# Small gaps inside the SBUF buffers that TensorE reads, in an attention and FP4 block on one core

## What is computed

```python
x  = L0_attn_src
xn = _layernorm(x, axis=-1)
# attention, per head: Q = elu(xn @ Wq + bq) + 1, K the same with Wk, v = xn @ Wv + bv
KV = jnp.einsum('bshd,bshm->bhdm', K, v)
Z  = 1.0 / (jnp.einsum('bshd,bhd->bsh', Q, K.sum(axis=1)) + EPS)
o  = jnp.einsum('bshd,bhdm,bsh->bshm', Q, KV, Z).reshape(b, s, H * DH)
x1 = _layer_norm(xn + o @ Wo + bo, g1, be1)
y  = jax.nn.gelu(x1 @ W1 + b1, approximate=False) @ W2 + b2
s  = _layer_norm(x1 + y, g2, be2)
# gated part; fp4_linear rounds both operands, blockwise
h  = jax.nn.silu(fp4_linear(xn, w_gate)) * fp4_linear(xn, w_up)
g  = _silu(fp4_linear(h, w_down))
out = x + s * g
```

## The kernel before, in words

| step | moving | columns | stationary | matmuls of `mm3` in all |
|---|---|---|---|---|
| `q_proj`, Q | `xnTh`, `xnTl` | 512 | `wqh`, `wql` | 768 |
| `at_step`, attention out | `Mh`, `Ml` | 256 | `RH[j]`, `RL[j]` | 1536 |
| `h_proj`, hidden layer | `xTh`, `xTl` | 512 | `w1h`, `w1l` | 768 |
| `f_step`, second layer | `w2h`, `w2l` | 256 | `RH[j]`, `RL[j]` | 1536 |
| `gate_up` | `wgh`, `wgl` | 352 | `xqh`, `xql` | 1536 |
| `down` | `wdh`, `wdl` | 256 | `hqh`, `hql` | 960 |

## Time and profile before

### The profile page before, as it was taken

The page is one execution under the profiler, slowest core; times in us unless marked ns, Lnnn a source line. Parts: engine busy times, 40 slices in busy tenths (PEclk is TensorE's granted clock), DMA queues, the critical chain, the costliest instruction groups (busy, mean ns, idle before and its releaser), DMA issues.

```text
span 1678.5 us, 30547 instructions
## 1 busy us (share of the span) xinstructions
PE 1644.1 (98%) x11105; PEld 1469.2 (88%) x11105; DVE 1322.8 (79%) x2587; ACT 967.5 (58%) x1754; POOL 778.4 (46%) x718
## 2 busy tenths in 40 slices
PE   7999999999999999999999999999999999999997
PEld 6878888888889898989999998989898999999897
DVE  6685664555879797979889797979797988979797
ACT  6665656655464646565655556464646565555644
POOL 4564543434134444444453534444444446353446
PEclk9999999999999999999999999999999999999999
DMA  7322323422200101021010102010101201010100
GB/s 230 130 77 89 106 66 116 121 91 91 93 1 1 51 1 51 19 86 52 1 51 2 51 2 104 2 51 2 51 19 34 77 29 51 1 51 2 51 1 26
DMA packets 69986, 89.36 MB, mean 53 GB/s; under 512 B 8383, under 2 KB 54603, under 8 KB 68814
## 3 DMA queue, kind: packets, MB, share of 16 engines
q1 hardware_dynamic: 69838, 87.42, 15.9%
HBM read 53.30 MB, written 34.10 MB: 52 GB/s over the span
## 4 chain that ended last, share of the span: by engine, by line
PE 54%; DVE 12%; issue 4%; ACT 1%; POOL 1%; DVEq 0%; ACTq 0%
PE QH L81 7%; PE QH L83 6%; PE QH L82 6%; PE AC L81 6%; PE AC L83 6%; PE AC L82 6%; PE GU L81 4%; PE GU L83 4%; PE GU L82 4%; PE TT L816 3%; DVE hb L1760 1%; DVE bslna L1840 1%; DVE hb L1758 1%; PE QH L714 1%; DVE AC L1831 1%
## 5 line engine op out<-in xcount | busy, mean ns | idle before, releaser
L1212 ACT ACTIVATE rh<-QH 128x512 fp32r<-128x512 f32 x256 | 147.1, 595 | 84.2 <-DVE QH L1918 80.1
L81 PE MATMUL GU<-wgh,xqh 128*128 128x352 f32 x512 | 171.2, 334 | 8.9 <-DVE hb L1760 8.8
L2416 POOL TENSOR_TENSOR hb<-hb,rs_h 128x704 f32<-128x704 f32 x64 | 89.1, 1392 | 170.0 <-DVE rs_h L1767 170.0
L82 PE MATMUL GU<-wgl,xqh 128*128 128x352 f32 x512 | 165.7, 324 | 0.0
L83 PE MATMUL GU<-wgh,xql 128*128 128x352 f32 x512 | 165.6, 323 | 0.0
L1933 DVE TENSOR_TENSOR rl<-QH,rh 128x512 fp32r<-128x512 f32 x128 | 85.7, 689 | 95.1 <-ACT rh L1212 74.7
L81 PE MATMUL AC<-Mh,rh 128*128 128x256 f32 x512 | 145.7, 285 | 0.0
L81 PE MATMUL AC<-w2h,rh 128*128 128x256 f32 x512 | 144.2, 282 | 0.0
L82 PE MATMUL AC<-Ml,rh 128*128 128x256 f32 x512 | 142.8, 279 | 0.0
L83 PE MATMUL AC<-Mh,rl 128*128 128x256 f32 x512 | 142.7, 279 | 0.0
L82 PE MATMUL AC<-w2l,rh 128*128 128x256 f32 x512 | 142.4, 278 | 0.0
(11 more groups left out here) (241 smaller groups left out, 5711.1 us busy)
## 6 DMA issues: line engine op xcount, KB each, us to landing
xa<-in_L_attn_src SPq DMA_DIRECT2D x16, 512.0 KB, 4.2
xt_scratch<-xth SPq DMA_DIRECT2D x32, 256.0 KB, 2.6
xt_scratch<-xtl SPq DMA_DIRECT2D x32, 256.0 KB, 3.0
xb<-in_L_attn_src SPq DMA_DIRECT2D x16, 512.0 KB, 4.2
xnTh<-xt_scratch SPq DMA_DIRECT2D x32, 256.0 KB, 4.7
xnTl<-xt_scratch SPq DMA_DIRECT2D x32, 256.0 KB, 5.4
out<-x SPq DMA_DIRECT2D x15, 512.0 KB, 6.6
m_scratch<-mh SPq DMA_DIRECT2D x16, 256.0 KB, 2.4
```

Of the source, the lines that this page charges most:

```text
L81: e.matmul(outp, lh, rh, start=start, stop=False, skip_group_check=check)
L82: e.matmul(outp, lh, rl, start=False, stop=False, skip_group_check=check)
L1212: e.activation(RH[j % 4][:], src, ACT.Copy).then_inc(S[sem], 1)
L2416: e.tensor_tensor(hb, hb, spread(rs_h[i % 2][:], 44), ALU.mult).then_inc(S["hin"], 1)
```

## The change

The buffers that TensorE reads get unused bytes inside. A new helper `spaced` allocates rows of `n + gap` numbers and hands out the first `n` of each. `gap` is in float32 numbers, so that 8 is 32 bytes. The slots of the two rings become 520 numbers long, of which 512 are used. `main_rest` shrinks from 682 to 562 numbers, since the space after it is full.

```diff
+        def spaced(name, k, n, gap):
+
+            return sb(name, [128, k, n + gap], F32R)[:, :, 0:n]
+
         sb("before_weights", [128, 24])
-        wqh, wql = sb("wqh", [128, 2, 1024], F32R), sb("wql", [128, 2, 1024], F32R)
-        w1h, w1l = sb("w1h", [128, 2, 1024], F32R), sb("w1l", [128, 2, 1024], F32R)
-        w2h, w2l = sb("w2h", [128, 8, D], F32R), sb("w2l", [128, 8, D], F32R)
-        wgh, wgl = sb("wgh", [128, 2, 1408], F32R), sb("wgl", [128, 2, 1408], F32R)
-        wdh, wdl = sb("wdh", [128, 6, D], F32R), sb("wdl", [128, 5, D], F32R)
+        wqh, wql = spaced("wqh", 2, 1024, 0), spaced("wql", 2, 1024, 0)
+        w1h, w1l = spaced("w1h", 2, 1024, 8), spaced("w1l", 2, 1024, 0)
+        w2h, w2l = spaced("w2h", 8, D, 0), spaced("w2l", 8, D, 0)
+        wgh, wgl = spaced("wgh", 2, 1408, 8), spaced("wgl", 2, 1408, 0)
+        wdh, wdl = spaced("wdh", 6, D, 0), spaced("wdl", 5, D, 0)
         sb("after_weights", [128, 8])
...
-        xnTh, xnTl = sb("xnTh", [128, 2, 512], F32R), sb("xnTl", [128, 2, 512], F32R)
+        xnTh, xnTl = spaced("xnTh", 2, 512, 16), spaced("xnTl", 2, 512, 8)
...
-        xqh, xql = sb("xqh", [128, 2, D], F32R), sb("xql", [128, 2, D], F32R)
+        xqh, xql = spaced("xqh", 2, D, 8), spaced("xql", 2, D, 24)
...
-        sb("main_rest", [128, 682])
+        sb("main_rest", [128, 562])
...
-        xTh, xTl = sb("xTh", [128, 2, 512], F32R), sb("xTl", [128, 2, 512], F32R)
+        xTh, xTl = spaced("xTh", 2, 512, 0), spaced("xTl", 2, 512, 8)
         Gb = sb("Gb", [128, 4, D])
-        RH = [sb(f"rh{i}", [128, 512], F32R) for i in range(4)]
-        RL = [sb(f"rl{i}", [128, 512], F32R) for i in range(4)]
-        hqh, hql = sb("hqh", [128, 6, 128], F32R), sb("hql", [128, 6, 128], F32R)
+        RH = [sb(f"rh{i}", [128, 520], F32R)[:, 0:512] for i in range(4)]
+        RL = [sb(f"rl{i}", [128, 520], F32R)[:, 0:512] for i in range(4)]
+        hqh, hql = spaced("hqh", 6, 128, 8), spaced("hql", 6, 128, 0)
```

## The result

The changed kernel takes 1687.39 us, the median of five runs (1686.94 to 1689.59), against 1679.61 us. The ratio is 1.0045, 95% interval 1.003 to 1.006: slower, by 7.8 us. The span of the profiled execution is 1685.5 us, 7.0 us longer.

What follows compares the result with a forecast made beforehand. TensorE, busy 98% of the span, was taken as the bound. Gains of 3.0 + 3.1 + 1.5 = 7.6 us, 74% of them reaching the end, gave 5.6 us less: 1674.0 us, range 1663 to 1687.

Steps and rivals of the forecast that it cites:

- The place: TensorE's matmuls, whose paces from start to start were expected to change with the distances between their operands.
- what reaches the end: Share of TensorE's gain that shortens the whole time: 74%, since 26% of a group runs through VectorE and ScalarE.
- The copies: Copies into `hqh`, `xqh` and `xql`, now written in several pieces: cost 0, at most 0.5 us before a waiting TensorE.
- the first phase: Opening matmuls of 512 columns, 226.4 ns each: distances stay 0, cost 0.
- The sign: Whole kernel: faster, 5.6 us less, with chances faster 0.49, same 0.22, slower 0.29.
- `f_step` and `down`: Their 2624 matmuls of 256 columns: no change, bounds 6.9 us more and 4.6 us less on TensorE.
- `at_step`: Its 1344 slow matmuls of 256 columns: 3.0 us less on TensorE, bounds 5.9 less and 0.8 more.
- `q_proj`: Its 768 matmuls of 512 columns go from 233.3 to 229.2 ns: 3.1 us less on TensorE.
- `gate_up`: Its 1536 matmuls of 352 columns: 1.5 us less on TensorE, bounds 6.6 less and 6.3 more.
- `h_proj`: Its 768 matmuls of 512 columns: no change, bounds 2.2 us less and 3.1 us more.
- The slower rival: Mixed distances break the good pace in `f_step`, `down`, `h_proj`: 10.0 us more on TensorE, 1687.0 us; chance 0.30.
- Nothing happens: Matmul paces depend on when a burst starts, not on addresses: time stays 1679.6 us; chance 0.20.

Runs made afterwards that it cites:

- the rings alone: Kernel before the change with only the ring slots lengthened to 520 numbers, 512 of them used; 1684.47 us, ratio 1.0029.
- the low parts moved: Kernel before the change with `Ml` and `w2l` 64 bytes further from `Mh` and `w2h`; one run, 1686.4 us against 1680.37.
- the steady 0: Kernel before the change with 64 unused bytes ahead of the rings, giving `at_step`, `f_step` and `down` distance 0 modulo 128; 1688.28 us, ratio 1.0047.
- the exchange of `q_proj` and `h_proj`: Kernel before the change with their distances exchanged, `q_proj` steady at 64 and `h_proj` at 96 modulo 128; 1682.99 us, ratio 1.0025.

## Why the prediction was wrong

*The place* was right, and so was what reaches the end: only TensorE's matmuls changed, in the mean of a step by some 3 ns at most, and 70% of it reached the span where I had 74%. The copies cost nothing, and the first phase kept its pace.

*The sign was wrong, and the step that failed is the one on `f_step` and `down`*: "I take no change, since half of the slots get distances like the good ones and half do not". They cost 5.4 and 3.4 us of busy time, half of the 17.6 us between the 7.6 less that I had on TensorE and the 10.0 more that came. Most of the other half is the gain of 7.6 us in `at_step`, `q_proj` and `gate_up`, of which at most 0.8 came; `h_proj` adds 2.4. I had counted 0 among the good distances because the first phase, with 512 columns, has it. At 256 columns 0 is bad, steady or not: 119.4 and 118.9 ns. So are 32 (119.1) and 96 (119.3). The distance that all of these steps had before, 64, is the only one of the four at which a whole step was seen at 113.3 ns: at 0, 32 and 96 no single `at_step`, `f_step` or `down` has a mean under 117 ns in the runs with a steady distance or with the rings alone. Three slots in four lost it.

*`at_step`*, 3.0 us less: 0.6. It rested on the distance modulo 256, "every second one is of the kind that `down` has". That is true of slot 1 alone, since the other slots no longer have 64 modulo 128; and moving `Mh` by 128 bytes, alone, changed nothing.

*`q_proj`*, 3.1 us less: 0.4 by the means, 0.2 in busy time. A steady distance of 64 or 0 does give 2.3 to 3.1 ns. The changed kernel keeps 96 in half of the product and mixes 0 and 32 in the other.

*`gate_up`*, 1.5 us less: 2.2 more by the means, 0.6 in busy time. *`h_proj`*, no change: 2.5 us more; both steady 96 and 0 (with 128 modulo 256) cost it about as much as the mixture.

*The slower rival* named the steps `f_step`, `down` and `h_proj`, 10.0 us on TensorE and 1687.0 us; busy time rose by 10.0 and the time is 1687.39. The places were right. That the sum meets the tenth is luck: the three cost 11.2, and the other matmuls gave back 1.2. Its reason, that a changing distance keeps the streams from settling, is half of it. The run with the low parts moved shows, as far as one run can, that such a mixture harms; the rings alone and the steady 0 show that a wrong distance harms as much with no mixture within a step. My chances gave it 0.30 against 0.42, and counted against it that "within one slot of the ring the distance modulo 128 stays". That was a true objection to its reason, and none to its time.

*Nothing happens* falls: in the exchange of `q_proj` and `h_proj`, the paces went with the distances. What I had drawn from the rule of the Trainium skill, "TensorE: Matmul & The Clock Gate", section "Step-by-step: what each phase is for", on the two independent read ports, falls with it: that the addresses would not matter at all. Whether the rule itself fails, that the load of the next weights takes nothing from the matmul that streams, no run here shows, since it is still inference that it is this load which the stream meets. In the kernels with a steady distance the stationary operand of a matmul and that of the next have the same address modulo 128, so that the two can't be told apart, and none was run that could.

Also open is what one step hands to the next. `at_step` went from 117.1 to 114.8 ns when modulo 128 only `q_proj` had been given another distance, and to 114.6 when `gate_up` and `down` had; but its own distance modulo 256 went from 64 to 192 in both.

## What to carry to other kernels

Where TensorE is the bound and its matmuls follow each other without a gap, measure the time from start to start for each step, and compare it with the fastest for its width: here the steps of the main phase with 256 and 512 columns lay 17.7 us above the fast pace by the table of means (1.1% of the time), and placement alone moved the time by 0.5% up and 0.2% down. Look for a good distance between moving and stationary buffer for each width of its own (in this kernel 64 modulo 128 bytes for 256 columns of fp32r, and 64 or 0 modulo 256 for 512), and give it to all three matmuls of a product and to all slots of a ring: sizes that are multiples of 128 bytes keep it, and gaps of 32 to 96 bytes inside the buffers destroy it. Move the beginning of a buffer rather than its inside, note what lies behind it and moves along, and read all steps again, since a step whose distance modulo 128 was not touched can move by 2 ns.

## What was not expected of the hardware

- Equal matmuls run at paces that differ by up to 6.7 ns, with nothing changed but addresses: 113.3 and 120.0 ns for 256 columns, 226.7 and 233.3 for 512. Of the 6.7, 4.4 occur within one kernel and one distance (113.3 and 117.7).
- The good distance depends on the width: 0 modulo 128 gives 119 ns at 256 columns and, as 0 modulo 256, 226.7 at 512. At 352 columns the means of all that was tried lie between 160.0 and 161.4 ns.
- A pace outlives the step: with 64, a whole `at_step` holds 113.3 or 117.5 ns by what ran before it.
